# A state-space layer with an FP4 feed-forward block: x kept split in SBUF, batches 2 and 3 prepared inside the tile loop, down projection in 17 passes

## Chip, cores and metric

The kernel runs on one core of a Trainium2 chip. The metric is device time in microseconds (us) of one execution, the median of several runs.

## What is computed

The input x is 4 batches of 2048 positions of 256 features, float32. The reference, cut to what matters (the learned weights are A, B, C, D, gamma, beta and three feed-forward matrices):

```python
xB = einsum('bsh,nh->bsn', x, B); xD = einsum('bsh,oh->bso', x, D)
state_t = state_{t-1} @ A.T + xB_t                 # 16 states, 2048 steps, per batch
out = layernorm(einsum('bsn,hn->bsh', states, C) + xD) * gamma + beta
x   = layernorm(x + out)
gate, up = fp4_linear(x, w_gate), fp4_linear(x, w_up)      # 256 -> 704
y   = fp4_linear(silu(gate) * up, w_down)                  # 704 -> 256
return layernorm(x + y)
```

`fp4_linear` quantizes both its operands in blocks of 16 along the contracted dimension (scale = largest magnitude / 6, eight grid values) and multiplies the dequantized values in full precision.

## The kernel before, in words

**Precision.** TensorE's fp32r passes are used in threes: an operand is split into a part `Hi` (a cast to fp32r) and a part `Lo` (value minus `Hi`), and a product is Hi·Hi + Hi·Lo + Lo·Hi (`split_products`, line 1009 is its matmul). Plain float32 matmuls are used for the chunk states, the chain of links and all transposes.

**The front.** A tile is 128 rows of x (one position out of each of 128 chunks of 8 positions); there are 64 tiles, 16 per batch. Before the tile loop the kernel transposes all of x in 32 units of four 128x128 transposes (`x_transposes`, L915; copied by ScalarE to `xT`, L528), quantizes the weights in six pieces (VectorE `w_scales` and `w_round`, L702 to L712; GpSimd L431, L438; ScalarE L534) and turns them in ten groups (L928, L932, then `w_hi` L540 and `w_lo` L719). It also computes the states at the chunk ends: `chunk_states` (L941, 16 float32 matmuls of 256 columns per batch, over `xT`), then the chain `link(p, k)`, k = 0 to 8, for a pair of batches at once. Link 0 is seven matmuls (L959), links 1 to 6 and 7 are one each (L965 to L971), link 8 is eight (L977); VectorE answers each of links 0 to 7 with one small operation (L728 to L738). Pair 0 is finished in the front; batch 3's chunk states stand around the first layers, and pair 1's nine links stand in a row after step 1.

**The tile loop.** Every engine runs one list of operations per step, each with a lag in tiles (`run`); the list's order is the order on the engine, and semaphores tie the engines together. Two groups of eight steps are written out, the rest is a hardware loop of six rounds of eight steps. In TensorE's order one step is:

- `h_turn` (L1062): six transposes of the quantized hidden rows; ScalarE's `h_hi` (L630) and VectorE's `h_lo` (L838) split the result.
- `gu1`, `gu2` (L1009): 6 passes of 512 and 6 of 384 columns of gate and up; then `x_turn` (L1030), two transposes.
- `layer` (L1020, L1009): 1 + 6 passes of 256 columns into the bank `yb`.
- `ffn_down` (L1009): 18 passes of 256 columns into `turned`; VectorE's `add_x1` (L845) reads it.
- `gu0` (L1009): 6 passes of 512 columns.

For `layer`, SyncE's queue copies the tile's columns of `xT` to `xtTile`, ScalarE's `t_hi` (L609) and GpSimd's `t_lo` (L465) split them into `tHi`, `tLo`. VectorE's list holds, in this order, `x_scale` (L781), `h_lo` (L838), `x_recip`, `h_sum` (L828), `times_up` (L809), `h_grid`, `x_lo`, `h_max`, `add_x1` (L845), `h_scale`, `x_sum`, `h_recip` (L823) and more. GpSimd's `h_norm` (L480) follows `h_recip`.

## Time and profile before

| quantity | value |
|---|---|
| median of 3 runs | 611.5 us (610.8 to 612.59) |
| the profiled execution's own time | 613.03 us |
| span of its profile | 611.2 us |
| PE (TensorE matmul) busy | 579.6 us (95%), 3705 instructions |
| DVE (VectorE) busy | 514.5 us (84%), 1226 |
| ACT (ScalarE) busy | 472.2 us (77%), 1422 |
| POOL (GpSimd) busy | 466.2 us (76%), 604 |
| mean granted TensorE clock | 0.975 |
| DMA queue of SP | 46144 packets, 37.99 MB, 20.5% of 16 engines |

Busy times of an engine are the union of its instructions. Matmuls overlap one another in the records, so what a pass costs is read from the distance between starts, not from its duration. The granted clock is that of TensorE as a share of 2.4 GHz. In the timeline a bracket behind a row is idle time of the engine before it and what ended it.

### The profile page before, as it was taken

To read this page: it belongs to the slowest core of one execution; us is meant where nothing else is said; L and a number is where in the kernel's file an instruction comes from. 1 tells how busy PE (TensorE), PEld (TensorE's weight loads), DVE (VectorE), ACT (ScalarE), POOL (GpSimd) and SP (SyncE) were. 2 spreads that over 40 slices of the span, in tenths; PEclk is the share of its full clock that TensorE was granted. 3 is DMA by queue.
4 is the path that set the end of the run, shared out by engine and by line. 5 is a ranking of instruction groups with operands and counts; after the bars stand their busy time and mean duration, and the time that the engine had idled before them with its cause. 6 is when DMAs were issued, how large, how long until landed. Compare 5 with 4: busy or idle time off the path is not lost.

```text
span 611.2 us, 12675 instructions
## 1 busy us (share of the span) xinstructions
PE 579.6 (95%) x3705; PEld 521.4 (85%) x3705; DVE 514.5 (84%) x1226; ACT 472.2 (77%) x1422; POOL 466.2 (76%) x604
## 2 busy tenths in 40 slices
PE   5999966899999999999999999999999999999984
PEld 4777855799999999999999999999999999999874
DVE  2695115999999999999999999999999999999971
ACT  3445327778888888888888888888888888888763
POOL 1461126988888888888898888888888888888642
PEclk9999966999999999999999999999999999999997
DMA  6734021111112112111111111111111111100001
GB/s 235 291 109 137 22 57 40 47 40 38 56 56 56 56 56 56 56 55 55 55 55 55 55 54 54 52 53 52 55 55 55 54 55 55 54 27 17 19 20 41
DMA packets 46171, 38.32 MB, mean 63 GB/s; under 512 B 6912, under 2 KB 44864, under 8 KB 45120
## 3 DMA queue, kind: packets, MB, share of 16 engines
q1 hardware_dynamic: 46144, 37.99, 20.5%
q8 instruction: 13, 0.21, 0.1%
q14 instruction: 14, 0.11, 0.1%
HBM read 19.50 MB, written 8.39 MB: 46 GB/s over the span
## 4 chain that ended last, share of the span: by engine, by line
PE 92%; ACT 3%; DVE 2%; issue 1%; POOL 1%; DMA 1%; POOLq 0%; ACTq 0%
PE gu L1009 40%; PE turned L1009 22%; PE yb L1009 7%; PE turned L1062 7%; PE gu L941 3%; PE turned L941 2%; PE turned L1030 2%; PE yb L915 2%; PE gu L915 2%; PE yb L1020 1%; DMA scratch<-in_L_attn_x_dram 1%; PE turned L977 1%; ACT xT L528 1%; ACT htHi L630 0%; PE grid L968 0%
## 5 line engine op out<-in xcount | busy, mean ns | idle before, releaser
L1009 PE MATMUL gu<-wguHi,xtHi 128*128 128x512 f32 (+1 forms) x384 | 150.8, 393 | 2.1 <-DVE xtLo L802 2.0
L1009 PE MATMUL gu<-wguLo,xtHi 128*128 128x512 f32 (+1 forms) x384 | 145.4, 379 | 0.0
L1009 PE MATMUL gu<-wguHi,xtLo 128*128 128x512 f32 (+1 forms) x384 | 145.2, 378 | 0.0
L480 POOL TENSOR_TENSOR scratch<-scratch 128x704 f32<-128x704 f32 x64 | 92.3, 1442 | 34.9 <-DVE scratch L823 34.9
L1009 PE MATMUL turned<-wdHi,htHi 128*128 128x256 f32 x384 | 110.4, 287 | 3.8 <-DVE htLo L838 3.8
L1009 PE MATMUL turned<-wdHi,htLo 128*128 128x256 f32 x384 | 109.8, 286 | 0.0
L1009 PE MATMUL turned<-wdLo,htHi 128*128 128x256 f32 x384 | 108.9, 284 | 0.0
L485 POOL TENSOR_TENSOR scratch<-scratch 128x704 f32<-128x704 f32 x64 | 88.9, 1388 | 9.5 <-DVE scratch L833 9.4
L630 ACT CAST htHi<-turned 128x768 fp32r<-128x768 f32 x64 | 51.3, 802 | 42.1 <-PE turned L1062 42.1
L1009 PEld LDWEIGHTS gu<-wguHi,xtHi 128*128 128x128 f32 x384 | 72.9, 190 | 12.1 <-DVE xtLo L802 2.8
L1009 PEld LDWEIGHTS gu<-wguHi,xtLo 128*128 128x128 f32 x384 | 72.4, 189 | 11.4
L1009 PEld LDWEIGHTS gu<-wguLo,xtHi 128*128 128x128 f32 x384 | 73.0, 190 | 9.1
L1009 PEld LDWEIGHTS turned<-wdHi,htHi 128*128 128x128 f32 x384 | 73.5, 191 | 4.2 <-DVE htLo L838 4.2
L1009 PEld LDWEIGHTS turned<-wdLo,htHi 128*128 128x128 f32 x384 | 74.5, 194 | 0.0
L1009 PEld LDWEIGHTS turned<-wdHi,htLo 128*128 128x128 f32 x384 | 73.2, 191 | 0.0
L838 DVE TENSOR_TENSOR htLo<-turned,htHi 128x768 fp32r<-128x768 f32 x64 | 61.3, 958 | 13.2 <-ACT htHi L630 6.1
L465 POOL TENSOR_TENSOR tLo<-xtTile,tHi 128x256 fp32r<-128x256 f32 x64 | 47.3, 739 | 17.0 <-ACT tHi L609 17.0
L809 DVE TENSOR_TENSOR scratch<-scratch,gu 128x704 f32<-128x704 f32 x64 | 56.0, 874 | 1.8 <-PE gu L1009 1.8
L833 DVE SCALAR_TENSOR_TENSOR scratch<-grid,scratch 128x704 f32<-128x704 f32 x64 | 56.6, 884 | 0.0
L813 DVE TENSOR_REDUCE gu<-scratch 128x44 f32<-128x704 f32 x64 | 56.5, 883 | 0.0
L1062 PEld LDWEIGHTS turned<-ident,scratch 128*128 128x128 f32 x384 | 45.6, 140 | 10.8 <-POOL scratch L485 1.4
L1062 PE MATMUL turned<-ident,scratch 128*128 128x128 f32 x384 | 52.4, 273 | 1.9 <-POOL scratch L485 1.2
(171 smaller groups left out, 1560.5 us busy)
## 6 DMA issues: line engine op xcount, KB each, us to landing
scratch<-in_L_attn_x_dram SPq DMA_DIRECT2D x8, 1024.0 KB, 5.2
xtTile<-xT SPq DMA_DIRECT2D x64, 128.0 KB, 2.3
scratch<-in_L_attn_x_dram SPq DMA_DIRECT2D x64, 128.0 KB, 2.4
out_dram<-scratch SPq DMA_DIRECT2D x64, 128.0 KB, 1.9
stTile<-statesHi SPq DMA_DIRECT2D x128, 8.0 KB, 1.7
stTile<-statesLo SPq DMA_DIRECT2D x64, 8.0 KB, 1.7
scratch<-in_L_ffn_w_down_dram SPq DMA_DIRECT2D x1, 704.0 KB, 7.5
scratch<-in_L_ffn_w_up_dram SPq DMA_DIRECT2D x1, 640.0 KB, 6.0
```

What stands on the lines that cost most here:

```text
L465: nc.gpsimd.tensor_tensor(tLo[:, m % 2, :, :], xtTile[:, m % RING, :, :], as_f32(tHi[:, m % 2, :, :]), ALU.subtract).then_inc(s_tlo, 1)
L480: nc.gpsimd.tensor_tensor(blocks(hx[:, m % 2, :]), blocks(hx[:, m % 2, :]), each_block(hRc[:, m % 4, :], FB), ALU.mult).then_inc(s_xnh, 1)
L485: nc.gpsimd.tensor_tensor(blocks(hq[:, m % 2, :]), blocks(hq[:, m % 2, :]), each_block(hSc[:, m % 4, :], FB), ALU.mult).then_inc(s_qh, 1)
L630: nc.scalar.copy(htHi[:, m % 2, :, :].rearrange("p c k -> p (c k)"), ht).then_inc(s_hi, 1)
L809: nc.vector.tensor_tensor(hx[:, m % 2, :], silu[:, m % 2, :], gu[:, FF:GU], ALU.mult).then_inc(s_h, 1)
L813: nc.vector.tensor_reduce(amH, blocks(hx[:, m % 2, :]), AX_X, ALU.max, apply_absolute_value=True).then_inc(s_ham, 1)
L833: nc.vector.scalar_tensor_tensor(out=hq[:, m % 2, :], in0=hm, scalar=LEAST, in1=hx[:, m % 2, :], op0=ALU.max, op1=ALU.subtract, reverse1=T ...
L838: nc.vector.tensor_tensor(htLo[:, m % 2, :, :].rearrange("p c k -> p (c k)"), ht, as_f32(htHi[:, m % 2, :, :]).rearrange("p c k -> p (c k) ...
L915: ins = nc.tensor.transpose(to[:, q * P:(q + 1) * P], xRaw[:, h % 2, (t * KH + q) * P:(t * KH + q + 1) * P], ident[:, :])
L941: ins = nc.tensor.matmul(fBank[b // BPP][:, b % BPP * CPB:(b % BPP + 1) * CPB], gPad[:, c, N * t:N * t + P], xT[:, t, c, b * CPB:(b + 1) * ...
L1009: ins = nc.tensor.matmul(to, l, r, start=(first and q == 0), stop=(q == len(passes) - 1))
L1062: ins = nc.tensor.transpose(ht[:, q * P:(q + 1) * P], hq[:, m % 2, row:row + P], ident[:, :])
```

## The change

Five things change together.

1. `xT`, `xtTile`, `tHi`, `tLo` and the operations `t_hi`, `t_lo`, `load_columns` go. Transposed x is kept as `xHi` and `xLo` in fp32r, with room for two batches; `layer` reads them in place. In the front ScalarE writes `xHi` (`x_hi_first`) and VectorE `xLo` (`x_lo_first`), for 16 units instead of 32.
2. Tile 32 + k is loaded (`xNext`), transposed, split and stored inside the loop, in step k + 1, for k = 0 to 31, so in steps 1 to 32 (`next_turn` on TensorE into the second half of bank `yb`, `next_hi` on ScalarE, `next_lo` on VectorE). In these steps `layer` waits for the `next_lo` of the same step.
3. `chunk_states` uses three fp32r passes per product: 48 passes of 256 columns per batch. Batch 0's stand in the front, batch 1's in steps 0 and 1, batch 2's in steps 14 to 17, batch 3's in steps 30 to 33. The chain of links runs per batch (32 columns): batch 0's in the front, batch 1's one link a step in steps 3 to 11, batch 2's in 19 to 27, batch 3's in 35 to 43.
4. The down projection has 17 passes: its last 64 rows are stacked twice (`hTail`, `wTwice`), so that two passes do what three did. GpSimd's `h_scale` becomes two instructions (640 and 128 columns).
5. The hardware loop is gone: all steps are written out, and the front's order is a hand-written list on each engine.

The core of the diff:

```diff
+    AHEAD = 2 * PER_BATCH
+    STATES_AT = {0: (1, range(0, 4)), 1: (1, range(4, CHUNK))}
+    LINK_AT = {3 + k: (1, k) for k in range(LINKS)}
+    for b_ in range(2, BATCH):
+        first_ = PER_BATCH * (b_ - 2) + 14
+        STATES_AT.update({first_ + q: (b_, (2 * q, 2 * q + 1)) for q in range(CHUNK // 2)})
+        LINK_AT.update({first_ + 5 + k: (b_, k) for k in range(LINKS)})
...
-        xT = sb("xT", [P, CHUNK, KH, CHUNKS])
+        xHi = sb("xHi", [P, 2, CHUNK, KH, CPB], F32R)
+        xLo = sb("xLo", [P, 2, CHUNK, KH, CPB], F32R)
...
+        xp = yb[:, H:2 * H]
...
+            def next_lo(h, m):
+                k = h * CHUNK + m - 1
+                if not 0 <= k < TILES - AHEAD:
+                    return
+                slot, t, col = place(AHEAD + k)
+                dve.wait_ge(s_ph, k + 1)
+                nc.vector.tensor_tensor(xLo[:, slot, t, :, col:col + P], xp.rearrange("p (c k) -> p c k", c=KH),
+                                        as_f32(xHi[:, slot, t, :, col:col + P]), ALU.subtract).then_inc(s_pl, 1)
...
-            run(dve, [(x_grid, 2), (scale_gamma, 0), (x_max, 1), (add_x, 0), (x_scale, 1), (h_lo, 5), (x_recip, 1),
-                      (h_sum, 4), (times_up, 3), (h_grid, 4), (x_lo, 2), (h_max, 3), (add_x1, 5), (h_scale, 3),
-                      (x_sum, 1), (h_recip, 3)],
+            run(dve, [(x_grid, 3), (scale_gamma, 1), (x_max, 2), (add_x, 1), (states_rest, 1), (x_scale, 2), (chain, 0),
+                      (h_lo, 6), (x_recip, 2), (h_sum, 5), (next_lo, 0), (times_up, 4), (h_grid, 5), (x_lo, 3),
+                      (h_max, 4), (add_x1, 6), (h_scale, 4), (x_sum, 2), (h_recip, 4)])
...
+            def chunk_states(b, positions):
...
+                for t in positions:
+                    ins = split_products(f_bank(b), [((gHi[:, c, N * t:N * t + P], gLo[:, c, N * t:N * t + P]),
+                                                      (xHi[:, b % 2, t, c, :], xLo[:, b % 2, t, c, :]))
+                                                     for c in range(KH)], first=(t == 0), last=(t == CHUNK - 1), skip=True)
...
             def layer(h, m):
...
-                pe.wait_ge(s_tlo, done(h, m))
                 pe.wait_ge(s_ld[r], 3 * done_dma(h, m))
-                if not isinstance(tile, int) or tile >= 1:
+                if tile >= 1:
                     pe.wait_ge(s_x1p, done(h, m - 1))
+                    pe.wait_ge(s_pl, min(tile, TILES - AHEAD))
...
+            def next_turn(h, m):
+                step = h * CHUNK + m
+                k = step - 1
+                if not 0 <= k < TILES - AHEAD:
+                    return
+                pe.wait_ge(s_ldn[k % RING], 16 * (k // RING + 1))
+                pe.wait_ge(s_x1p, step)
+                for c in range(KH):
+                    ins = nc.tensor.transpose(xp[:, c * P:(c + 1) * P], xNext[:, k % RING, c * P:(c + 1) * P], ident[:, :])
+                ins.then_inc(s_pt, 1)
...
                 split_products(db, [((htHi[:, m % 2, q, :], htLo[:, m % 2, q, :]), (wdHi[:, q, :], wdLo[:, q, :]))
-                                    for q in range(NKD)]).then_inc(s_dn, 1)
+                                    for q in range(NKD - 1)], last=False)
+                nc.tensor.matmul(db, htHi[:, m % 2, NKD - 1, :], wdHi[:, NKD - 1, :], start=False, stop=False)
+                nc.tensor.matmul(db, htLo[:, m % 2, NKD - 1, :], wdLo[:, NKD - 1, :], start=False,
+                                 stop=True).then_inc(s_dn, 1)
...
-            run(pe, [(h_turn, 6), (gu1, 4), (gu2, 4), (x_turn, 3), (layer, 0), (ffn_down, 6), (gu0, 3)],
+            run(pe, [(h_turn, 6), (chain, 0), (gu1, 4), (next_turn, 0), (gu2, 4), (x_turn, 3), (layer, 0), (ffn_down, 6),
+                     (next_states, 0), (gu0, 3)])
```

How the change moves instructions, at the two places that the prediction speaks of. First TensorE in one step of the loop, from `gu2` to the start of `layer`, before:

```order
L1009 MATMUL gu<-wguHi,xtHi 128x384 [waits s_hsc]
L1009 MATMUL gu<-wguLo,xtHi 128x384
L1009 MATMUL gu<-wguHi,xtLo 128x384
L1009 MATMUL gu<-wguHi,xtHi 128x384
L1009 MATMUL gu<-wguLo,xtHi 128x384
L1009 MATMUL gu<-wguHi,xtLo 128x384
L1026 REGISTER_ALU
L1030 MATMUL turned<-ident,scratch 128x128 [waits s_lo,s_qx]
L1030 MATMUL turned<-ident,scratch 128x128
L1016 REGISTER_ALU
L1017 ISA [waits s_tlo]
L1020 MATMUL yb<-cStack,stTile 128x256 [waits s_x1p,s_ld0]
```

and now, in a step that prepares a tile:

```order
L1082 MATMUL gu<-wguHi,xtLo 128x512
L1212 MATMUL yb<-ident,xNext 128x128 [waits s_x1p,s_ldn0]
L1212 MATMUL yb<-ident,xNext 128x128
L1082 MATMUL gu<-wguHi,xtHi 128x384 [waits s_hsc]
L1082 MATMUL gu<-wguLo,xtHi 128x384
L1082 MATMUL gu<-wguHi,xtLo 128x384
L1082 MATMUL gu<-wguHi,xtHi 128x384
L1082 MATMUL gu<-wguLo,xtHi 128x384
L1082 MATMUL gu<-wguHi,xtLo 128x384
L1243 MATMUL turned<-ident,scratch 128x128 [waits s_lo,s_qx]
L1243 MATMUL turned<-ident,scratch 128x128
L1198 MATMUL yb<-cStack,stTile 128x256 [waits s_pl,s_x1p,s_ld1]
```

Two transposes of `xNext` into `yb` stand ahead of `gu2`, and the first matmul of `layer` waits for `s_pl` (set by `next_lo`) where it waited for `s_tlo`. Second VectorE in one step, from `x_scale` on, before:

```order
L781 TENSOR_SCALAR xSc<-xAm 128x16 [waits s_xam]
L838 TENSOR_TENSOR htLo<-turned,htHi 128x768 [waits s_hi]
L786 RECIPROCAL xRc<-xSc 128x16 [waits s_xsc]
L828 SCALAR_TENSOR_TENSOR scratch<-grid,scratch 128x704 [waits s_mh]
L809 TENSOR_TENSOR scratch<-scratch,gu 128x704 [waits s_up,s_silu]
L833 SCALAR_TENSOR_TENSOR scratch<-grid,scratch 128x704 [waits s_hsum]
L802 TENSOR_TENSOR xtLo<-turned,xtHi 128x256 [waits s_xhi]
L813 TENSOR_REDUCE gu<-scratch 128x44 [waits s_h]
```

and now:

```order
L920 TENSOR_SCALAR xSc<-xAm 128x16 [waits s_xam]
L977 TENSOR_TENSOR htLo<-turned,htHi 128x768 [waits s_hi]
L925 RECIPROCAL xRc<-xSc 128x16 [waits s_xsc]
L967 SCALAR_TENSOR_TENSOR scratch<-grid,scratch 128x704 [waits s_mh]
L896 TENSOR_TENSOR xLo<-yb,xHi 128x2x128 [waits s_ph]
L948 TENSOR_TENSOR scratch<-scratch,gu 128x704 [waits s_up,s_silu]
L972 SCALAR_TENSOR_TENSOR scratch<-grid,scratch 128x704 [waits s_hsum]
L941 TENSOR_TENSOR xtLo<-turned,xtHi 128x256 [waits s_xhi]
```

`next_lo` (L896, `xLo<-yb,xHi`) stands behind `h_lo` (L977) and `h_sum` (L967) and ahead of `times_up` (L948); it waits for `s_ph`, set by ScalarE's `next_hi`.

## Rows read from the trace of the kernel before

**Rows 1.** Windows: stretch, its length, busy us of each engine, granted clock, DMA.

```profile
200.00:300.00 100.00, 100.00 (x662) 91.96 (x662) 95.13 (x233) 88.00 (x272) 89.73 (x117) 1.00 0.19 55
```

**Rows 2.** Chain of work that ended last: two down projections; start, us, what.

```profile
119.55 2.16 PE turned L1009 x18
...
552.61 2.16 PE turned L1009 x18
```

**Rows 3.** Timeline of TensorE, one step: start us, us, engine, line, op, out<-in.

```profile
300.81 0.82 PE L1062 MATMUL turned<-ident,scratch 128*128 128x128 f32 x6
...
303.94 0.38 PE L1030 MATMUL turned<-ident,scratch 128*128 128x128 f32 x2
304.07 0.36 PE L1020 MATMUL yb<-cStack,stTile 128*128 128x256 f32 x1
...
304.98 0.29 PE L1009 MATMUL turned<-wdHi,htHi 128*128 128x256 f32 x1
...
307.14 0.40 PE L1009 MATMUL gu<-wguHi,xtHi 128*128 128x512 f32 x1
...
308.55 0.82 PE L1062 MATMUL turned<-ident,scratch 128*128 128x128 f32 x6
```

**Rows 4.** Timeline of ScalarE, the same step.

```profile
301.67 0.80 ACT L630 CAST htHi<-turned 128x768 fp32r<-128x768 f32 x1 [0.43 <-PE turned L1062]
...
303.08 0.76 ACT L617 ACTIVATE scratch<-gu 128x704 f32<-128x704 f32 x1
```

**Rows 5.** Timeline of VectorE, the same step.

```profile
302.08 0.30 DVE L781 TENSOR_SCALAR xSc<-xAm 128x16 f32<-128x16 f32 x1
302.50 0.96 DVE L838 TENSOR_TENSOR htLo<-turned,htHi 128x768 fp32r<-128x768 f32 x1
...
303.54 0.83 DVE L828 SCALAR_TENSOR_TENSOR scratch<-grid,scratch 128x704 f32<-128x704 f32 x1
304.28 0.87 DVE L809 TENSOR_TENSOR scratch<-scratch,gu 128x704 f32<-128x704 f32 x1
...
307.34 0.42 DVE L845 SCALAR_TENSOR_TENSOR scratch<-turned,scratch 128x256 f32<-128x256 f32 x1 [0.26 <-PE turned L1009]
```

**Rows 6.** Timeline of VectorE, where TensorE waits for it in the fill.

```profile
106.39 0.42 DVE L802 TENSOR_TENSOR xtLo<-turned,xtHi 128x256 fp32r<-128x256 f32 x1
```

**Rows 7.** Timeline of TensorE, the matmul that waited for it.

```profile
106.86 0.50 PE L1009 MATMUL gu<-wguHi,xtHi 128*128 128x512 f32 x1 [0.34 <-DVE xtLo L802]
```

**Rows 8.** Timeline of TensorE in the front: links 0 and 1 of pair 0.

```profile
48.12 1.90 PE L959 MATMUL gu<-fLast,sRev 16*128 16x64 f32 x14
...
50.96 0.28 PE L965 MATMUL gu<-enter,power 16*16 16x64 f32 x2
```

**Rows 9.** Windows of the front and the fill.

```profile
10.00:48.00 38.00, 36.99 (x216) 28.93 (x214) 31.20 (x47) 18.33 (x52) 17.27 (x12) 1.00 0.54 192
48.00:72.00 24.00, 23.40 (x154) 19.48 (x153) 7.54 (x19) 11.17 (x24) 2.64 (x4) 1.00 0.23 68
70.00:100.00 30.00, 20.48 (x103) 16.56 (x103) 7.81 (x27) 9.69 (x32) 10.96 (x18) 0.71 0.20 51
```

**Rows 10.** Timeline of VectorE in the front: one subtraction of 512 columns.

```profile
47.81 0.68 DVE L719 TENSOR_TENSOR wguLo<-turned,wguHi 128x512 fp32r<-128x512 f32 x1
```

**Rows 11.** Timeline of TensorE: layers 0, 1, 2 and the first h_turn.

```profile
72.72 0.36 PE L1020 MATMUL yb<-cStack,stTile 128*128 128x256 f32 x1
...
79.00 0.36 PE L1020 MATMUL yb<-cStack,stTile 128*128 128x256 f32 x1 [1.75 <-POOL tLo L465]
...
93.30 0.55 PE L1020 MATMUL yb<-cStack,stTile 128*128 128x256 f32 x1 [2.38 <-DVE scratch L770]
...
115.23 0.81 PE L1062 MATMUL turned<-ident,scratch 128*128 128x128 f32 x6
```

**Rows 12.** Timeline of GpSimd: h_norm of the same step.

```profile
300.90 1.45 POOL L480 TENSOR_TENSOR scratch<-scratch 128x704 f32<-128x704 f32 x1 [0.55 <-DVE scratch L823]
```

**Rows 13.** Timeline of TensorE in the front: one float32 chunk-states batch of 16 products.

```profile
38.93 7.07 PE L941 MATMUL gu<-xT,gPad 128*128 128x256 f32 x32
```

More of the change, by code:

```diff
@@ new lines, in _ @@
+            w_round(1)
+            x_lo_first(6)
+            w_scales(2)
+            x_lo_first(7)
+            link(0, 0)
+            w_lo(0)
+            link(0, 1)
+            x_lo_first(8)
+            w_round(2)
+            link(0, 2)
+            w_lo(1)
+            link(0, 3)
+            x_lo_first(9)
+            w_scales(3)
+            link(0, 4)
+            w_lo(2)
+            link(0, 5)
+            x_lo_first(10)
+            w_round(3)
+            link(0, 6)
+            w_lo(3)
@@ new lines, in _, with chain @@
+            link(0, 7)
+            x_lo_first(11)
+            w_scales(4)
+            states_lo(0)
+            w_round(4)
+            w_lo(4)
+            x_lo_first(12)
+            w_scales(5)
+            w_lo(5)
+            x_lo_first(13)
+            w_round(5)
+            w_lo(6)
+            x_lo_first(14)
+            w_lo(7)
+            x_lo_first(15)
+            w_lo(8)
+            w_lo(9)
+            dve.wait_ge(s_bcast, 32)
+            def chain(h, m):
+                b, k = LINK_AT.get(h * CHUNK + m, (0, LINKS - 1))
+                if k < LINKS - 1:
+                    link(b, k)
@@ new lines, in w_transposes, with split_products @@
+                        pe.wait_ge(s_wtwice, k + 1)
+                        ins = nc.tensor.transpose(to[:, q * P:(q + 1) * P], wTwice[:, k, :], ident[:, :])
+                ins.then_inc(s_wt, 1)
+            def split_products(to, terms, first=True, last=True, skip=False):
+                passes = [(l, r) for (lh, ll), (rh, rl) in terms for l, r in ((lh, rh), (lh, rl), (ll, rh))]
+                for q, (l, r) in enumerate(passes):
+                    ins = nc.tensor.matmul(to, l, r, start=(first and q == 0), stop=(last and q == len(passes) - 1),
+                                           skip_group_check=skip)
+                return ins
@@ L1000, in _ @@
-            pe.wait_ge(s_xtc, 4 * HALVES)
-            pe.wait_ge(s_states, 1)
-            pe.wait_ge(s_wlo, len(W_GROUPS))
-            pe.wait_ge(s_cstack, 48)
-            def split_products(to, terms, first=True):
-                passes = [(l, r) for (lh, ll), (rh, rl) in terms for l, r in ((lh, rh), (lh, rl), (ll, rh))]
-                for q, (l, r) in enumerate(passes):
-                    ins = nc.tensor.matmul(to, l, r, start=(first and q == 0), stop=(q == len(passes) - 1))
-                return ins
+            pe.wait_ge(s_small, 64)
@@ new lines, in _ @@
+            x_transposes(6)
+            powers(9)
+            chunk_states(0, (4, 5))
+            x_transposes(7)
+            powers(10)
+            chunk_states(0, (6, 7))
+            w_transposes(0)
+            x_transposes(8)
+            link(0, 0)
+            w_transposes(1)
+            link(0, 1)
+            x_transposes(9)
+            link(0, 2)
+            w_transposes(2)
+            link(0, 3)
+            x_transposes(10)
+            link(0, 4)
+            w_transposes(3)
```

602 lines of the change are left out of this document (351 added, 251 removed).

## The prediction

> **What bounds the kernel now.** I read the windows first. In a stretch of 100 us in the tile loop TensorE is busy for all of it, VectorE for 95.13, the others for less [rows 1]. The chain of waits says the same: it runs along TensorE, and the down projections of tiles 1 and 57 start 433.06 us apart, 7.733 us a step [rows 2]. One step in the timeline shows no pause on TensorE: h_turn at 300.81, the next at 308.55 [rows 3]. The reader should see two more things there. ScalarE waits 0.43 us for h_turn before h_hi [rows 4], and VectorE's h_lo starts 0.03 us after h_hi has ended (301.67 + 0.80; 302.50) [rows 4, 5]. So a path leads from h_turn over ScalarE and VectorE. Today nothing early in TensorE's step hangs on its end. Before the loop there is a front, in which TensorE is 97% busy, and a fill in which nobody is: 20.48 of 30 us for TensorE, at a granted clock of 0.71 [rows 9]. The first h_turn starts at 115.23 [rows 11].
>
> **The change, part by part.** Times count from h_turn = 0 in a step.
>
> *Down projection.* 18 passes take 307.14 - 304.98 = 2.16 us, 0.12 each [rows 3]; one goes: -0.12 a step. GpSimd's second h_scale instruction lies beside this; GpSimd loses t_lo for it and has room [rows 1].
>
> *The tile ahead, TensorE's part.* Two transposes with the switch of operands cost what x_turn costs: x_turn and layer take 304.98 - 303.94 = 1.04 us, of which seven passes are 0.84, so 0.20 [rows 3]. If that were all, a step would be 7.733 - 0.12 + 0.20 = 7.81 us.
>
> *The tile ahead, the wait.* Layer now waits for next_lo of its own step, and next_lo stands behind h_lo and h_sum. That path is fixed by rows: h_turn to h_hi 0.86 (301.67), to h_lo 1.69 (302.50), to h_sum 2.73 (303.54), and to the next place on VectorE 3.47 (304.28) [rows 3 to 5]. next_lo is a 256-column subtraction from PSUM like x_lo, 0.42 [rows 6]: its end is at 3.89. TensorE starts 0.05 after such an end (106.81 to 106.86) [rows 6, 7]. next_hi is no later: silu starts at 2.27 [rows 4], is followed within some 0.75 by next_hi, and that ends near 3.4. So layer starts at 3.94, where it could have started at 304.07 - 300.81 + 0.20 = 3.46. Behind it come layer 0.91, 17 passes 2.04 and gu0 1.41 [rows 3]: the step is 8.30 us, +0.56. Queued behind the waiting matmul are down, gu0 and the next h_turn, so nothing on TensorE fills the gap, and the path closes on itself. The bounds are 8.25 (VectorE reaches next_lo a little earlier) and 8.40. In steps 1 to 32 a tile is prepared; 27 of these follow the first h_turn (steps 6 to 32): 27 x 0.56 = +15.1. VectorE's and ScalarE's new operations have their price in this path; the loads of `xNext` take the place of `xtTile`'s on SP's queue, four tiles ahead, and cost nothing unless they land over two steps late.
>
> *Steps 33 to 63.* Only the shorter down projection is left: 31 x -0.12 = -3.7.
>
> *Chunk states of batches 2 and 3.* Eight steps carry 12 passes of 256 columns each between down and gu0, that is on the closed path: 96 x 0.12 = +11.5.
>
> *Links.* No row shows a float32 matmul of 32 columns. With 64 columns seven take 1.90 us, 0.27 each, and one of link 1 takes 0.28 [rows 8]. Bounds: half of that (columns decide) and all of it (the weight load decides). I take the middle, 0.19: link 0 costs 1.3, link 8 1.5, the seven between about 0.1 each of TensorE's time ahead of gu1. Two batches in full and links 3 to 8 of batch 1: 2 x 3.5 + 1.9 = 8.9, less 0.4 for what the wait before layer hides: +8.5, bounds +4 and +12.
>
> *The front.* TensorE loses 16 units of x and most chunk states there, but VectorE gains work. It was busy 31.20 + 7.54 = 38.7 us up to 72 [rows 9]; it gains 16 subtractions of 512 columns at 0.65 (0.68 less the overlap) [rows 10] and one of the pad, 11 in all. From 10 us on that is 60 if it never idles. It will: link 0 of batch 0 needs the eighth x_lo, 12 passes, a copy and seven matmuls (some 4.5 us), and the last weight piece goes round over GpSimd, ScalarE and TensorE (some 4). I put layer 0 at 68.5 where it was at 72.72 [rows 11]. Then the fill: layers 0, 1, 2 were 6.3 and 14.3 us apart, the second with pair 1's nine links between [rows 11]; now both take about 5.8, as only the normalization of the tile before and next_lo stand there. From layer 2 to the first h_turn it took 21.9; I add 0.5 for each of three steps: 23.4. The first h_turn comes at 68.5 + 11.5 + 23.4 = 103.4: -12. Bounds: -20 (VectorE never idle) and -3 (the gain of the fill alone, half of it lost).
>
> *The written-out program.* Steps 0 to 15 are written out already, and from tile 1 to tile 57 the cadence of 7.733 holds through them and all the loop's rounds [rows 2]: 0. The Trainium skill (Runtime: NRT & Kernel Launch, instruction fetch mechanics) says that a taken branch outside the fetched window stalls the fetch and prefers unrolling; by that rule each of five back-branches would give something back, but the cadence shows none.
>
> **Sum.** -12 + 15.1 - 3.7 + 11.5 + 8.5 = +19.4 us. The profiled execution's own time is 613.03 for a span of 611.2, so 1.8 lies around the span and stays; the median of the runs shown is 611.5, 1.5 below that execution. I put the sum on the median: **631 us**. The terms' bounds give 616 to 647.
>
> **The rivals.**
>
> *A, the path stays open* (chance 0.12). VectorE reaches next_lo in time, and a step costs TensorE's work only, 7.81: 27 x 0.08 = 2.2 in place of 15.1, so 618. For it: VectorE idles 0.26 us before add_x1 [rows 5]. Against: that idle time lies behind next_lo and can't move ahead of it.
>
> *B, the front runs at TensorE's pace* (0.10), the case on the other side. Place: before layer 0. TensorE is 97% busy there. It loses three float32 batches at about 7 us [rows 13] and 16 units at about 0.5, some 29 us; if VectorE's work fits beside, layer 0 stands near 43, 26 earlier than in my sum: 605. It decides once the first h_turn comes more than 31 us earlier than now, before 84. Against it: VectorE alone has 50 us of work.
>
> *C, a second path over GpSimd is longer than the first* (0.11). add_x1 comes 0.20 behind down: at 7.09. From it to h_norm's end it is 2.75 (307.34; 300.90 + 1.45, one step on) [rows 5, 12], where x_scale ends too (302.08 + 0.30) [rows 5]; then h_lo can start at 9.9, and needs to at 8.30 + 1.69 = 9.99. The slack is 0.1. Were it overrun by 0.3 a step, 27 x 0.3 = +8: 639. The Trainium skill (SBUF — State Buffer, two separate sides) says a VectorE instruction in a two-port mode and a GpSimd one exclude each other for a whole instruction; x_scale ending with h_norm agrees.
>
> **How the numbers follow.** My forecast has 0.67. Its own range is 616 to 647, with little at the ends; A and C lie in or at it, B is left out. I give 612 to 644. What this kernel's measurement can tell from no change is about 0.3%, 1.8 us. Faster by more: B and a sliver, 0.12. Within: 0.05. Slower by more: 0.83.
>
> **What would show it.** In the changed profile layer waits for next_lo near 0.48 us in each of steps 6 to 32, and h_turns stand 8.3 apart there, 9.7 in steps with chunk states, 7.61 from step 33 on. The first h_turn is near 103, layer 0 near 68. Steps of 7.8 mean A, a first h_turn before 84 B, steps of 8.6 with ScalarE's h_hi ended long before h_lo C. I am wrong if the front gives back more than 20 us, or if link 0 and link 8 cost nothing.

## The result and the profile after

The changed kernel takes 647.08 us (median of 4 runs, 645.9 to 647.64), the kernel before beside it 611.86: ratio 1.0575, 95% interval 1.0554 to 1.0596. It is slower, as forecast, but by 35 us where the forecast had 19, and outside the range. The page of the changed kernel begins so (busy us, share of the span, instructions; then busy tenths in 40 slices; then the chain of work that ended last, by engine):

```profile
span 645.8 us, 12093 instructions
...
PE 589.7 (91%) x3793; PEld 525.0 (81%) x3793; DVE 533.4 (83%) x1293; ACT 459.5 (71%) x1377; POOL 445.2 (69%) x608
...
PE   4666688999999999999999999999999999999974
...
PE 73%; DVE 14%; ACT 7%; issue 2%; POOL 2%; DMA 1%; SPq 0%; POOLq 0%; ACTq 0%; DVEq 0%
```

VectorE and ScalarE hold 21% of that chain: the path no longer runs along TensorE alone. One preparing step (a step that prepares a tile) without links or chunk states, on TensorE, to be read against [rows 3]; rows are left out where the same kind of matmul goes on:

```profile
219.86 0.82 PE L1281 MATMUL turned<-ident,scratch 128*128 128x128 f32 x6
...
221.92 0.38 PE L1212 MATMUL yb<-ident,xNext 128*128 128x128 f32 x2
...
223.20 0.38 PE L1243 MATMUL turned<-ident,scratch 128*128 128x128 f32 x2
223.88 0.36 PE L1198 MATMUL yb<-cStack,stTile 128*128 128x256 f32 x1 [0.31 <-DVE xLo L896]
...
224.79 0.28 PE L1082 MATMUL turned<-wdHi,htHi 128*128 128x256 f32 x1
...
226.80 0.40 PE L1082 MATMUL gu<-wguHi,xtHi 128*128 128x512 f32 x1
...
228.19 0.82 PE L1281 MATMUL turned<-ident,scratch 128*128 128x128 f32 x6
```

And VectorE and ScalarE in that step, to be read against [rows 4, 5]:

```profile
221.55 0.96 DVE L977 TENSOR_TENSOR htLo<-turned,htHi 128x768 fp32r<-128x768 f32 x1 [1.54 <-ACT htHi L704]
...
222.58 0.83 DVE L967 SCALAR_TENSOR_TENSOR scratch<-grid,scratch 128x704 f32<-128x704 f32 x1
223.32 0.41 DVE L896 TENSOR_TENSOR xLo<-yb,xHi 128x256 fp32r<-128x256 f32 x1
```

```profile
220.71 0.80 ACT L704 CAST htHi<-turned 128x768 fp32r<-128x768 f32 x1 [1.69 <-PE turned L1281]
...
222.12 0.76 ACT L691 ACTIVATE scratch<-gu 128x704 f32<-128x704 f32 x1
...
222.87 0.37 ACT L682 CAST xHi<-yb 128x256 fp32r<-128x256 f32 x1
```

The step is 228.19 - 219.86 = 8.33 us. next_lo starts at 3.46 after h_turn and ends at 3.87 (forecast 3.47 and 3.89); layer starts at 4.02 (forecast 3.94). Layer's row shows 0.31 us of idle time, but a row's idle time counts from the modelled end of the matmul before. By starts layer comes 0.68 us behind x_turn, where in [rows 3] it came 0.13 behind (303.94; 304.07): the wait costs about 0.55.

The waits of 1.54 and 1.69 us further up are large because this step comes right behind one with chunk states, in which TensorE had 1.41 us more to do before h_turn. Where a plain step comes behind a plain one, they are smaller:

```profile
173.36 0.80 ACT L704 CAST htHi<-turned 128x768 fp32r<-128x768 f32 x1 [0.88 <-PE turned L1281]
...
174.19 0.96 DVE L977 TENSOR_TENSOR htLo<-turned,htHi 128x768 fp32r<-128x768 f32 x1
```

ScalarE waits 0.88 for h_turn, where before it was 0.43 [rows 4], and h_lo follows h_hi at once. A closed path looks like this: TensorE waits for VectorE in each step, ScalarE waits longer than before for TensorE, and no engine is busy all the time.

Where the 34.6 us of span come from (611.2 to 645.8), by the starts of the h_turns. A step is counted from its h_turn to the next; the first h_turn is that of step 6.

| part | forecast | measured |
| --- | --- | --- |
| up to the first h_turn (115.23, now 110.53) | -12 | -4.7 |
| wait and turn, 27 preparing steps (6 to 32) of 8.34 | +15.1 | +16.4 |
| chunk states, 8 steps of 9.75 | +11.5 | +11.3 |
| links (what steps have beyond 8.34, 9.75 or 7.55) | +8.5 | +15.8 |
| steps 33 to 63, 7.55 | -3.7 | -5.7 |
| from the h_turn of step 64 to the end (47.5, now 49.0) | 0 | +1.5 |

Two terms failed by 7 us each, the front and the links. The last steps are shorter than one pass less accounts for.

The first row is less certain than the others. Three runs below, whose instructions differ from this kernel's only from step 36 on (extra_pool, extra_act, extra_all), have their first h_turn at 109.0 to 109.2, not at 110.5. The section on the front shows where these 1.4 us come from.

### The profile page after: what moved, and what is told of

Its sections match the earlier page's. It is cut to its first block, busy times and chain, and to the rows that moved or that the text cites. A ratio compares the mean times of both kernels' runs of the same rounds, so it can differ in the third digit from the quotient of the medians.

```text
span 645.8 us, 12093 instructions
## 1 busy us (share of the span) xinstructions
PE 589.7 (91%) x3793; PEld 525.0 (81%) x3793; DVE 533.4 (83%) x1293; ACT 459.5 (71%) x1377; POOL 445.2 (69%) x608
## 3 DMA queue, kind: packets, MB, share of 16 engines
q1 hardware_dynamic: 32768, 29.60, 15.8%
## 4 chain that ended last, share of the span: by engine, by line
PE 73%; DVE 14%; ACT 7%; issue 2%; POOL 2%; DMA 1%; SPq 0%; POOLq 0%; ACTq 0%; DVEq 0%
PE gu L1082 29%; PE turned L1082 18%; PE yb L1082 7%; PE turned L1281 6%; DVE htLo L977 3%; PE grid L1082 3%; PE yb L1198 2%; ACT htHi L704 2%; DVE scratch L967 2%; DVE xLo L896 2%; ACT scratch L691 2%; PE turned L1292 1%; PE turned L1291 1%; PE turned L1243 1%; DVE xLo L820 1%
## 5 line engine op out<-in xcount | busy, mean ns | idle before, releaser
L503 POOL TENSOR_TENSOR scratch<-scratch 128x704 f32<-128x704 f32 x64 | 92.2, 1440 | 20.4 <-DVE scratch L962 20.1
L1082 PE MATMUL turned<-wdHi,htHi 128*128 128x256 f32 x320 | 91.8, 287 | 3.8 <-DVE htLo L977 3.8
L488 POOL TENSOR_TENSOR rs<-ve2t,neg_half 128x1 f32<-128x1 f32 x64 | 35.2, 550 | 82.9 <-ACT ve2t L642 82.9
L1082 PE MATMUL turned<-wdHi,htLo 128*128 128x256 f32 x320 | 91.4, 285 | 0.0
L1082 PE MATMUL turned<-wdLo,htHi 128*128 128x256 f32 x320 | 91.2, 285 | 0.0
L508 POOL TENSOR_TENSOR scratch<-scratch 128x640 f32<-128x640 f32 x64 | 82.2, 1284 | 10.2 <-DVE scratch L972 10.0
L977 DVE TENSOR_TENSOR htLo<-turned,htHi 128x768 fp32r<-128x768 f32 x64 | 61.2, 957 | 25.8 <-ACT htHi L704 23.1
L1082 PEld LDWEIGHTS turned<-wdHi,htHi 128*128 128x128 f32 x320 | 61.6, 193 | 4.4 <-DVE htLo L977 4.4
L1082 PEld LDWEIGHTS turned<-wdLo,htHi 128*128 128x128 f32 x320 | 61.7, 193 | 0.0
L1082 PEld LDWEIGHTS turned<-wdHi,htLo 128*128 128x128 f32 x320 | 61.7, 193 | 0.0
L948 DVE TENSOR_TENSOR scratch<-scratch,gu 128x704 f32<-128x704 f32 x64 | 56.2, 877 | 2.4 <-PE gu L1082 2.2
L691 ACT ACTIVATE scratch<-gu 128x704 f32<-128x704 f32 x64 | 48.0, 750 | 10.7 <-PE gu L1082 10.7
```

The source lines that it names most:

```text
L488: nc.gpsimd.tensor_tensor(dst[:, j:j + 1], src[:, j:j + 1], neg_half[:, :], ALU.pow).then_inc(signal, 1)
L503: nc.gpsimd.tensor_tensor(blocks(hx[:, m % 2, :]), blocks(hx[:, m % 2, :]), each_block(hRc[:, m % 4, :], FB), ALU.mult).then_inc(s_xnh, 1)
L508: nc.gpsimd.tensor_tensor(blocks(hq[:, m % 2, 0:KD[-1]]), blocks(hq[:, m % 2, 0:KD[-1]]), each_block(hSc[:, m % 4, 0:KD[-1] // BLOCK], KD[ ...
L691: nc.scalar.activation(silu[:, m % 2, :], gu[:, 0:FF], ACT.Silu).then_inc(s_silu, 1)
L948: nc.vector.tensor_tensor(hx[:, m % 2, :], silu[:, m % 2, :], gu[:, FF:GU], ALU.mult).then_inc(s_h, 1)
L977: nc.vector.tensor_tensor(htLo[:, m % 2, :, :].rearrange("p c k -> p (c k)"), ht, as_f32(htHi[:, m % 2, :, :]).rearrange("p c k -> p (c k) ...
```

## The experiments

Seventeen runs of sixteen kernels. Where a ratio is given, the kernel before ran on the same chip beside it (medians of 612.15 to 612.78 us). "After" is the changed kernel. Differences in us between two changed kernels are of medians that can come from different chips. The diffs are cut to what matters.

### The ring opened (ring_open)

The ring is the closed path: h_turn, h_hi, h_lo, h_sum, next_lo, layer, and behind layer the next h_turn.

```diff
-run(pe, [(h_turn, 6), (chain, 0), (gu1, 4), (next_turn, 0), (gu2, 4), (x_turn, 3), (layer, 0), (ffn_down, 6),
+run(pe, [(h_turn, 6), (chain, 0), (gu1, 4), (gu2, 4), (x_turn, 3), (layer, 0), (next_turn, 0), (ffn_down, 6),
 ...
-    pe.wait_ge(s_pl, min(tile, TILES - AHEAD))        # layer
+    pe.wait_ge(s_pl, min(tile - 1, TILES - AHEAD))
 ...
-    pe.wait_ge(s_x1p, step)                           # next_turn
+    act.wait_ge(s_pt, min(h * CHUNK + m, TILES - AHEAD))   # mean_square, from step 1
 ...
-(silu_gate, 4), (nm2, 1), (next_hi, 0), (x_hi, 3), (sq2, 1), (nr3, 9), (ve2, 1),
-(mean_square, 0), (x_abs, 2), (ve1, 0), (ve3, 8)])
+(silu_gate, 4), (nm2, 1), (x_hi, 3), (sq2, 1), (nr3, 9), (ve2, 1),
+(mean_square, 0), (next_hi, 0), (x_abs, 2), (ve1, 0), (ve3, 8)])
 ...
-(h_lo, 6), (x_recip, 2), (h_sum, 5), (next_lo, 0), (times_up, 4), (h_grid, 5), (x_lo, 3),
-(h_max, 4), (add_x1, 6),
+(h_lo, 6), (x_recip, 2), (h_sum, 5), (times_up, 4), (h_grid, 5), (x_lo, 3),
+(h_max, 4), (next_lo, 0), (add_x1, 6),
```

> The tile ahead is turned right behind layer, next_hi stands behind mean_square and next_lo behind h_max; layer no longer waits for a subtraction of its own step, and the transposes no longer stand ahead of gu2. Closed-path theory (my forecast's ring term): the plain preparing step falls from 8.34 to between 7.75 and 7.85 us (TensorE's own work: 7.55 plus 0.20 to 0.25 for the turn), 27 steps x 0.5 to 0.55 = 13.5 to 15 us less, and a link ahead of gu1 costs its own TensorE time only: 631 to 634 in all. Rival C (the path over GpSimd's h_norm sets the step): the step stays near 8.3 and the time near 647. Rival D (TensorE's own work grew by more than 0.2, the wait only covers it): the step falls by less than 0.2, time 642 or more.

Measured: 627.24 us, ratio to before 1.0252 (1.0224 to 1.028), 19.8 less than after. Plain preparing steps take 7.77 to 7.80, steps with one link 8.14, steps with chunk states 9.20. TensorE in a step with a link, and VectorE in the same step:

```profile
234.44 0.82 PE L1283 MATMUL turned<-ident,scratch 128*128 128x128 f32 x6
235.19 0.23 PE L1121 MATMUL gu<-carry,power 16*16 16x32 f32 x2
235.34 0.50 PE L1084 MATMUL gu<-wguHi,xtHi 128*128 128x512 f32 x1
...
237.90 0.38 PE L1245 MATMUL turned<-ident,scratch 128*128 128x128 f32 x2
238.04 0.37 PE L1201 MATMUL yb<-cStack,stTile 128*128 128x256 f32 x1
...
238.96 0.38 PE L1214 MATMUL yb<-ident,xNext 128*128 128x128 f32 x2
```

```profile
240.90 0.41 DVE L898 TENSOR_TENSOR xLo<-yb,xHi 128x256 fp32r<-128x256 f32 x1
```

The layer waits for nothing, and next_lo works 2.9 us behind it, in time VectorE had to spare. TensorE does the same work as in after. So the closed path was the cause: 14.2 us come back in the 27 steps. Rivals C and D are out. Another 4.5 come back before the first h_turn (106.0), which the expectation had left out: in the fill, too, the layers of after waited for next_lo, layers 1 and 2 for 1.01 us each, layers 3 to 5 for 0.58, 0.25 and 0.70. That is 3.6 us of waits in all; the rest of the 4.5 was not traced. The last 1 us lies behind the h_turn of step 64, where kernels differ without a cause that was found (see the tail below).

### The links left out (no_links) and halved (links_half)

```diff
 def chain(h, m):          # on TensorE and on VectorE
+    return
 ...
-    if k == LINKS - 1:
-        link(b, k)         # TensorE, next_states
 ...
-    act.wait_ge(s_st_ps, b + 1)        # ScalarE, states_hi
+    act.wait_ge(s_loc if b else s_st_ps, b + 1)
```

> All nine links of batches 1, 2 and 3 are left out on TensorE and VectorE, so the states that enter a super-chunk are missing there (the output differs from the reference); the two copies to statesHi and statesLo stay. If the +15.8 us that steps 6 to 32 show beyond 8.34 and the chunk states are the links: every step from 6 to 32 is 8.34 or 9.75, and the time falls by 14 to 18 us, to 629 to 633. If my forecast's price (8.5) were right and the rest of the long steps came from something else (DMAs of states, copies to statesHi/Lo), it falls by 7 to 10, and steps over 8.5 remain.

Measured: 632.91 us, ratio 1.0338 (1.0308 to 1.0369), 14.2 less than after. From step 7 on every preparing step is 8.33 to 8.34 or 9.75 to 9.76, but for two of 8.70 in which states_hi and states_lo stand, and steps 34 to 43 are 7.55. Step 6 is 8.80 with links or without, and step 44 is 7.68. So, without the links, 2 x 0.36, 0.46 and 0.13 of the 15.8 that the table books under links are still there, and 14.5 us go, which is what the span lost (645.8 to 631.3). The 0.46 of step 6 is not the link's. The 0.36 beside the copies shows only in this kernel: in after the copies stand in the steps of link 8, whose eight matmuls account for all that these steps take longer (links_half, below), and the steps behind them are 8.34. What costs in a link is seen in after, h_turn to gu1 with one link, and link 0:

```profile
255.59 0.82 PE L1281 MATMUL turned<-ident,scratch 128*128 128x128 f32 x6
256.34 0.23 PE L1119 MATMUL gu<-carry,power 16*16 16x32 f32 x2
256.50 0.50 PE L1082 MATMUL gu<-wguHi,xtHi 128*128 128x512 f32 x1
...
258.01 0.38 PE L1212 MATMUL yb<-ident,xNext 128*128 128x128 f32 x2
...
259.28 0.38 PE L1243 MATMUL turned<-ident,scratch 128*128 128x128 f32 x2
259.92 0.36 PE L1198 MATMUL yb<-cStack,stTile 128*128 128x256 f32 x1 [0.27 <-DVE xLo L896]
```

```profile
228.94 1.75 PE L1111 MATMUL gu<-fLast,sRev 16*128 16x32 f32 x14
230.62 0.50 PE L1082 MATMUL gu<-wguHi,xtHi 128*128 128x512 f32 x1
```

gu1 starts 0.91 after h_turn, without a link 0.57 (220.43 - 219.86): 0.34 for one float32 matmul. And little of it vanishes in layer's wait, which is still 0.27: gu1 ends later, so next_turn is later (258.01 - 255.59 = 2.42, above 221.92 - 219.86 = 2.06), and ScalarE, which waits for gu1 before silu, is later with next_hi. VectorE, done with h_sum, then waits for next_hi:

```profile
259.35 0.42 DVE L896 TENSOR_TENSOR xLo<-yb,xHi 128x256 fp32r<-128x256 f32 x1 [0.21 <-ACT xHi L682]
```

Layer starts 4.33 after h_turn and not 4.02. The link delays the path to layer as well as TensorE. Such a step takes 8.63, 0.29 more than a plain one; in steps 36 to 41, where layer waits for nothing, the link costs 0.37 (7.92 against 7.55). So the wait hides 0.08.

links_half asks what the matmuls themselves cost, on top of ring_open:

```diff
-for c in range(SUPER - 1):                 # link 0
+for c in range(SUPER - 1 if b == 0 else 3):
-for c in range(SUPER):                     # link 8
+for c in range(SUPER if b == 0 else 4):
```

> ring_open with link 0 in 3 float32 matmuls of 7 and link 8 in 4 of 8 for batches 1 to 3 (the output differs from the reference: sums over the positions in a super-chunk are cut short). If each float32 matmul of 32 columns costs its own 0.24 to 0.25 us on TensorE whatever it multiplies: the steps with link 0 fall from 9.67 to 8.7, those with link 8 from 9.58 to 8.6, and the whole by 0.98 x 5 = 4.9, and about 1 in the fill: 621.5 to 622.5. If the price of a link is mainly its chain of waits over VectorE (my 0.1 for a matmul): under 0.5 a step, 624.5 or more.

Measured: 621.69 us, ratio 1.0183 (1.0133 to 1.0234), 5.6 less than ring_open. The step with link 0 falls from 9.67 to 8.77, that with link 8 from 9.58 to 8.69: four matmuls are 0.90, 0.22 each, in both links. They cost TensorE's time one by one. The five steps account for 4.4 of the 5.6; another 1.8 stand before layer 0 (72.04 against 73.84), which the edit does not touch.

### The front: SyncE's order and TensorE's order (states_early, chunk_later)

```diff
+for m in range(RING):
+    load_states(0, m)
 sp.wait_ge(s_xt, 4 * 2 * 2)
```

> The first four tiles' states are loaded ahead of SyncE's wait for the sixteenth unit of x. If layer 0 is late by this queue alone at the end of the front, layer 0 comes 2.0 to 2.6 us earlier (74.1 to 71.5 to 72.1), right behind the last x_lo, and the time falls by as much: 644.5 to 645. If the fill's first layers wait for something else behind it (weights, GpSimd's pad), nothing or under 0.5 is seen at the first h_turn: 646.6 to 647.1.

Measured: 644.69 us, ratio 1.0537 (1.0503 to 1.0571), 2.4 less. The two intervals overlap (after: 1.0554 to 1.0596), so this gain is not clear of noise. Layer 0 starts at 69.95, 4.1 earlier and more than expected, but the first h_turn only 1.7 earlier (108.82): the fill behind it grew. Against extra_pool, which has after's front and was quicker in it (layer 0 at 72.31, first h_turn at 109.18), it is 2.4 and 0.4.

```diff
-chunk_states(0, (0, 1))
 x_transposes(5)
 powers(8)
+chunk_states(0, (0, 1))
 x_transposes(6)
 ...
```

Pairs (2, 3) and (4, 5) move by one unit in the same way; (6, 7) keeps its place.

> In TensorE's front every pair of batch 0's chunk states stands one unit of x later. Theory: VectorE idles in the front (4.6, 2.5 and more us) since the unit's transposes are queued behind chunk states that wait for VectorE's own x_lo; then its idle time up to 34 us falls by 3 to 6 us and layer 0 comes 2 to 5 us earlier: 642 to 645. Rival: link 0 needs the last chunk states in any order and the idle time only moves to it: layer 0 within 1 us of 74.1, 646 to 648.

Measured: 640.75 us, ratio 1.0473 (1.0441 to 1.0505), 6.3 less, a little more than the expectation's best. Layer 0 starts at 68.47, the first h_turn at 105.14 (110.53). VectorE's front in after, then in chunk_later:

```profile
22.68 0.68 DVE L820 TENSOR_TENSOR xLo<-yb,xHi 128x512 fp32r<-128x512 f32 x1
27.91 0.69 DVE L820 TENSOR_TENSOR xLo<-gu,xHi 128x512 fp32r<-128x512 f32 x1 [4.55 <-ACT xHi L558]
...
33.16 0.69 DVE L820 TENSOR_TENSOR xLo<-yb,xHi 128x512 fp32r<-128x512 f32 x1 [2.48 <-ACT xHi L558]
```

```profile
22.66 0.68 DVE L820 TENSOR_TENSOR xLo<-yb,xHi 128x512 fp32r<-128x512 f32 x1
23.26 0.68 DVE L820 TENSOR_TENSOR xLo<-gu,xHi 128x512 fp32r<-128x512 f32 x1
...
27.57 0.69 DVE L820 TENSOR_TENSOR xLo<-yb,xHi 128x512 fp32r<-128x512 f32 x1 [1.44 <-ACT xHi L558]
```

In after, unit 5's transposes stand on TensorE behind chunk states that wait for VectorE's x_lo of unit 4:

```profile
23.51 0.55 PE L1082 MATMUL turned<-xHi,gHi 128*128 128x256 f32 x1 [4.15 <-DVE xLo L820]
...
26.20 1.05 PE L1054 MATMUL gu<-ident,scratch 128*128 128x128 f32 x4
```

So ScalarE gets nothing to copy and VectorE nothing to subtract: each waits for the other through TensorE's queue. From 16 us to layer 0 VectorE waited 10.0 us in all for the copies of x in after, 3.2 in chunk_later.

Part of that is TensorE's pace. In after the first two groups of 12 chunk-state passes stand 0.213 us apart, the next two 0.118. The second and the third group, each with its four transposes:

```profile
28.75 0.55 PE L1082 MATMUL turned<-xHi,gHi 128*128 128x256 f32 x1 [1.28 <-DVE xLo L820]
...
31.45 1.05 PE L1054 MATMUL yb<-ident,scratch 128*128 128x128 f32 x4
...
34.00 0.36 PE L1082 MATMUL turned<-xHi,gHi 128*128 128x256 f32 x1 [1.28 <-DVE xLo L820]
...
35.49 0.60 PE L1054 MATMUL gu<-ident,scratch 128*128 128x128 f32 x4
```

A group begins 5.25 us behind the one before at the first pace (28.75 to 34.00) and 3.59 at the second (34.00 to 37.59). In extra_pool, with the same front, only the first group is slow, VectorE's subtraction at 33.16 stands at 31.54, and layer 0 comes at 72.31. That is the difference between executions named above. So of the 5.4 us by which chunk_later's first h_turn is earlier (105.14 against 110.53), 4.0 stand against extra_pool's 109.18. The record of the granted clock shows 1.00 in these microseconds, so it does not tell the two paces apart, and why TensorE was slow there is open.

All three edits together, ring_front:

> The changed kernel with the tile turned behind layer, the first states loaded ahead of the wait, and batch 0's chunk states one unit later, all three. If the savings add (19.8, 2.4 and 6.3 us): 618 to 620. If the front's two edits meet (in the kernel with later chunk states layer 0 waited 4.0 us for the states, in the one with early loads the fill grew by 2.5), they give 7 to 9 together, and the opened ring shortens the fill on its own: 617 to 621. Either way slower than before, since 8 x 1.41 of chunk states, links and 32 x 0.24 of turns stay on TensorE.

Measured: 621.64 us, ratio 1.014 (1.0122 to 1.0159). The first h_turn starts at 99.72, 6.3 before ring_open's. The time is just above the expected 617 to 621. The front's two edits give less together than apart: layer 0 starts at 66.00, and VectorE then waits for a one-column power of GpSimd, which is still at the weights:

```profile
71.24 0.49 DVE L906 SCALAR_TENSOR_TENSOR yb<-yb,rs,gamma_b 128x256 f32<-128x256 f32 x1 [4.16 <-POOL rs L490]
```

It is the best form of the whole change found, and 1.4% slower than the kernel before.

### The shorter last steps (before_17, before_out, before_17_out)

The forecast had 7.733 - 0.12 = 7.61 for a step without preparation; after shows 7.545. The two candidates were put into the kernel before, one by one and together. before_17 has the last chunk of the down projection stacked as in the change, with t_lo, t_hi and everything else as before; before_out is one line:

```diff
-PEELED = 2
+PEELED = HALVES          # and no eng.Fori
```

> The kernel before with the down projection in 17 passes alone (last chunk of 64 rows stacked twice, hTail written by a second instruction on GpSimd). Theory: one pass less on a TensorE that never pauses is 0.12 us a step, 64 steps: -7.0 to -7.9, a step of 7.61 in place of 7.733, 604 us. Rival: the second GpSimd instruction (0.40 us) meets the path h_norm, h_abs, h_sum there (GpSimd still has t_lo), and the gain is under half: 608 or more. Rival 2: the step is 7.545 here too, since the shorter step of the changed kernel comes from this pass alone: 600 us.

> The kernel before with all eight groups written out and no loop, nothing else changed. Theory (what the changed kernel's 7.545 us step is missing against 7.613): passes stand 0.118 apart instead of 0.120, so a step of 64 passes' worth is 7.65 to 7.67 in place of 7.733, all along or from the third group on, and the time falls by 3 to 5 us: 607 to 609. Rival (my forecast's): the written-out program gives nothing, 7.733, 611 to 613, and the shorter step comes from something else that left TensorE's queue.

> Both: 17 passes and written out, in the kernel before. If the two add, steps of 7.54 to 7.55 and 599 to 601 us; with no gain of the written-out form 604. This would be the quickest kernel so far, with none of the preparation inside the loop.

| kernel | median, us | ratio to before | a step, us |
| --- | --- | --- | --- |
| before_17 | 604.37 | 0.9856 (0.9838 to 0.9874) | 7.594 |
| before_out | 613.28 | 1.0003 (0.9987 to 1.002) | 7.733 |
| before_17_out | 605.15 | 0.9872 (0.9853 to 0.9891) | 7.594 |

Writing the program out gives nothing; my expectation for before_out fell and the forecast's zero stood, and with it the trace's word against the rule of the Trainium skill (Runtime: NRT & Kernel Launch, instruction fetch mechanics) that the prediction weighed. With 17 passes the step is 0.139 shorter, more than the forecast's 0.12: the down projection takes 2.04 where it took 2.16, and the gate and up passes 0.02 less in all. Another 0.05 is still missing.

### What stands beside TensorE (extra_pool, extra_act, extra_all)

The changed kernel no longer copies, subtracts and loads xtTile beside its last steps. Each of these was put back from step 36 on, for data nobody reads:

```diff
+if tile >= 36: nc.gpsimd.tensor_tensor(extraLo, beta_b, gamma_b, ALU.subtract)    # extra_pool
+if tile >= 36: nc.scalar.copy(extraHi, gamma_b)                                   # extra_act
+if tile >= 36: sp.dma_start(extraT[:, r, :, :], xHi[:, 0, j, :, 0:P])             # extra_all, with both
```

> The changed kernel; from step 36 on GpSimd does one more 256-column subtraction a step into a tile that nobody reads, where t_lo stood in the kernel before. Steps 45 to 63 now take 7.545 us, in the kernel before with 17 passes 7.594. If TensorE's passes stand closer since GpSimd touches the memory less: 7.57 to 7.60 in these steps, with no wait in them. If the 0.05 us has another cause (ScalarE's t_hi, the loads of xtTile, where the operands lie): 7.54 to 7.55 as before. If GpSimd becomes the bound: waits of layer or h_turn.

> The changed kernel; from step 36 on ScalarE does one more 256-column copy a step, where t_hi stood. If ScalarE's access makes the 0.05 us: steps 45 to 63 at 7.57 to 7.60 with no wait; if not, 7.54 to 7.55.

> The changed kernel; from step 36 on all three things that the kernel before did for its tile and the changed one no longer does are done beside it, for data that nobody reads: a load of 128 x 256 from another place in the memory beside the engines (as xtTile's), a 256-column copy on ScalarE, a 256-column subtraction on GpSimd. Alone, the last two left the step at 7.545. If traffic on that memory (the load, or all three) sets TensorE's pace: steps 45 to 63 at 7.58 to 7.60. If they stay at 7.54 to 7.55, the 0.05 us against 7.594 lies in nothing that this step does beside TensorE, and its cause stays open (what is left is where the operands lie, and what layer reads).

Measured, one run each: 645.33, 645.77 and 645.5 us, and a step of 7.545 in all three. GpSimd was busy 48.8 of 50 us in extra_pool and extra_all, and 54 GB/s moved in extra_all. This traffic costs TensorE nothing here, so the missing 0.05 has another cause.

### Where the operands lie (before_17_shift, after_shift, pad_896, pad_160)

```diff
+sb("pad", [P, 224])      # before_17_shift: 896 bytes a partition; after_shift: 288 columns
 scratch = sb("scratch", ...)
```

> The kernel before with 17 passes, and an unused tile of 896 bytes a partition in front of the scratch, so that the operands behind it (hq, xtHi, htHi and so on) lie at the same place modulo 1 KB as in the changed kernel. If where the operands lie sets the pitch of the passes: the step moves from 7.594 towards 7.545, or anywhere else by over 0.02. If not: 7.59 to 7.60.

> The changed kernel with an unused tile of 1152 bytes a partition in front of the scratch: what lies behind it now lies modulo 1 KB as in the kernel before with 17 passes. If where the operands lie sets the pitch: steps 45 to 63 move from 7.545 towards 7.594. If not: 7.54 to 7.55.

Measured, one run each: before_17_shift 603.5 us and a step of 7.545; after_shift 649.22 us, its last steps 7.62 and its preparing steps 8.37 (8.34). An unused tile changes every step, in both directions, and after_shift's goes past 7.594. Then the place was narrowed:

> before_17 with the 896 unused bytes right in front of xtHi and not in front of the scratch: only the stationary operands xtHi, xtLo, htHi, htLo (and stTile, tHi, tLo behind them) move, the scratch with hq and xm stays. If the place of the stationary operands decides: 7.54 to 7.55. If that of the scratch does (the transposes' operands, or what VectorE and the others read and write): 7.59 to 7.60.

> before_17 with 160 unused bytes in front of xtHi, so that the stationary operands begin at a multiple of 512 bytes a partition (704 and 224 past a multiple of 1024 and 512 were the two places so far: 864 slow, 736 quick). If a start on such a boundary is the best case: 7.545 or less, 601 or less. If the two places seen differ for another reason than alignment, the step may be anywhere between 7.5 and 7.65.

> before_17_shift once more, timed: it showed steps of 7.545 us at one look. Expected from that and before_17's 604.4: 63 x 0.05 = 3.1 less, 601 to 602 us, the quickest kernel here. If the one look was chance: 604.

| kernel | xtHi starts, modulo 512 bytes (from the declarations) | 17 down passes, us | a step, us | us |
| --- | --- | --- | --- | --- |
| before_17 | 352 | 2.04 | 7.594 | 604.37 |
| after_shift | 352 | 2.04 | 7.62 | 649.22 (one run) |
| after | 224 | 2.01 | 7.545 | 647.08 |
| before_17_shift | 224 | 2.01 | 7.545 | 602.31 (timed as shift_timed) |
| pad_896 | 224, scratch not moved | 2.01 | 7.56 to 7.58 | 600.91 (one run) |
| pad_160 | 0 | 2.00 | 7.57 | 604.52 |

The down projection of one step in before_17, its first, second and seventeenth matmul; then in before_17_shift:

```profile
499.23 0.29 PE L1029 MATMUL turned<-wdHi,htHi 128*128 128x256 f32 x1
499.35 0.28 PE L1029 MATMUL turned<-wdLo,htHi 128*128 128x256 f32 x1
...
501.15 0.28 PE L1094 MATMUL turned<-wdLo,htLo 128*128 128x256 f32 x1
```

```profile
497.68 0.28 PE L1030 MATMUL turned<-wdHi,htHi 128*128 128x256 f32 x1
497.80 0.28 PE L1030 MATMUL turned<-wdLo,htHi 128*128 128x256 f32 x1
...
499.57 0.28 PE L1095 MATMUL turned<-wdLo,htLo 128*128 128x256 f32 x1
```

Sixteen pitches take 1.92 us in the first, 1.89 in the second: 0.120 and 0.118 a pass. Moving xtHi, htHi and what lies behind them alone (pad_896) brings about half of the gain (7.56 to 7.58), with the down passes at 2.01 already; the other half came with the scratch, and lies in the gate and up passes (the 18 take 3.94 us in pad_896, 3.91 in before_17_shift). Pad_896's 600.91 us is one execution, whose first h_turn comes at 112.99 where before_17's is at 115.33, so its time says little; its step is longer than 7.545. A start on a multiple of 512 (pad_160) is not the best case, so the expectation's guess at a boundary fell. (Its "704 and 224" is a slip: 864 and 736 past a multiple of 1024 are 352 and 224 past one of 512.) Which property of the address decides is open. shift_timed has the lowest median of several runs here: ratio 0.983 (0.9807 to 0.9853), against 0.9856 (0.9838 to 0.9874) for before_17 and 0.986 (0.9834 to 0.9887) for pad_160. These intervals overlap, so the times alone don't tell the three apart; the steps do.

## Why the prediction was right and wrong

**Right: direction and the ring.** "Layer now waits for next_lo of its own step" and "the path closes on itself" was the largest term, +15.1; it measured +16.4, and ring_open took it away. The forecast step of 8.30 came out at 8.34: TensorE started 0.15 after next_lo's end and not 0.05, and the passes behind layer gave 0.05 back. Chunk states at 0.12 a pass were +11.5 and measured +11.3. Rivals A (7.81) and C (8.6, GpSimd) did not occur; B (a first h_turn before 84) neither.

**Wrong: the links, +8.5 and measured +15.8.** The step that failed is "the seven between about 0.1 each". I had [rows 8] with 0.28 for one float32 matmul of 64 columns and took 0.19 for 32, between half and all of it; the 0.1 for a single link is below even that and had no row behind it. Fewer columns hardly lower the price: link 0 is 1.75 for 32 columns and was 1.90 for 64, and one link costs TensorE 0.34 (its seven are 0.24 each). Link 0 cost 1.8 to 1.9 (forecast 1.3), link 8 1.8 (1.5), link 7 0.46 to 0.54, the others 0.29 in preparing steps and 0.37 behind them. The 0.4 that I took off for "what the wait before layer hides" was not the error: it hides 0.08 a link, some 0.9 in all. The other 0.46, in step 6, is no link's: no_links has it too.

**Wrong: the front, -12 and measured -4.7.** The step that failed is "I put layer 0 at 68.5"; it came at 74.10. The reasoning counted VectorE's work and two idle stretches, 4.5 for link 0 and 4 for the last weight piece. The first was 4.4 in the trace, but two more were missing: VectorE and TensorE waiting for each other around the chunk states (chunk_later: 4.0 to 5.4 us), and SyncE's loads of the first states, which stand behind its wait for the last unit of x and are issued from 71.08 on:

```profile
74.10 0.58 PE L1198 MATMUL yb<-cStack,stTile 128*128 128x256 f32 x1 [2.93 <-DMA stTile<-statesLo]
```

VectorE's work was smaller than I had it: it is busy 40.4 us from 10 us to layer 0, where the forecast had 50, and idle 23.7, where it had 8.5; besides the waits named, 2.3, 1.0, 2.0 and 1.2 us stand at weight pieces, a link and the states. So 68.5, which chunk_later meets at 68.47, would have been met by two errors that cancel. The rest, 1.5, is the fill: 36.4 us from layer 0 to the first h_turn, forecast 34.9.

The forecast also had no term for TensorE's clock in the front. Before it was 1.00 from 48 to 72 us [rows 9]; in after it was between the two levels, mostly at the lower (1.2 GHz):

```profile
48.00:72.00 24.00, 14.10 (x64) 12.03 (x64) 16.38 (x32) 9.64 (x18) 10.11 (x9) 0.53 0.03 6
```

TensorE, busy for 23.40 of these 24 us before, was busy for 14.10 after. Link 8 of batch 0 takes 3.6 us there, twice its 1.8 in the loop, and VectorE waits 1.95 for the states behind it. What this clock costs the front in all, no run shows: chunk_later and ring_front have it too (0.56 and 0.59 from 48 to 66 us).

**Wrong in size: the last steps, -3.7 and measured -5.7.** The term was "31 x -0.12". Seventeen passes are worth 0.139 at the old places (before_17), and the new places of the operands, which no row of before could show, 0.05 more.

**The tail, 0 and measured +1.5.** No cause was found. The stretch differs between kernels that do the same work there: before_out has 48.9 us behind the same h_turn, where before has 47.5, and the kernels with 17 passes have 47.1 to 49.1.

With the front and the links as measured the sum is 631 + 7.3 + 7.3 = 645.6; the tail's +1.5, the ring's +1.3, the last steps' -2.0 and the chunk states' -0.2 nearly cancel. The links came out beyond their own bound of +12, the front within its bound of -3; the range's upper end, 644, had cut both short, where the bounds together gave 647.
